# Moving the ending of the last state-space batch behind the phase boundary, and the first q and k loads in front of it

## The reference, cut to what matters

```
x1 = x  + layernorm(SSM(layernorm(x)))      # SSM: v + forward(v) + backward(v)
y  = x1 + layernorm(ATT(layernorm(x1)))     # ATT: attention, then 2 of 8 experts

forward(v): u, z = split(norm(v) @ Win.T); u = silu(conv4(u))
            dt, B, C from u;  h = exp(dt*A)*h + dt*u*B   (16 states, along the 512 positions)
            y = sum_n h_n*C_n + u*D;  out = (y * silu(z)) @ Wout.T
ATT(v):     q, k, v from rmsnorm(v); rope on q, k; 16 heads, 4 groups; causal softmax
            + residual; rmsnorm; router; the two chosen experts; + residual
```

## Times and profile before

| | us |
|---|---|
| median of 3 runs | 1732.66 |
| lowest, highest | 1731.58, 1736.15 |
| the profiled execution, its own time | 1733.05 |
| its span, from the first to the last instruction | 1731.3 |

### The profile page before, as it was taken

The page is one execution under the profiler, slowest core; times in us unless marked ns, Lnnn a source line. Parts: engine busy times, 40 slices in busy tenths (PEclk is TensorE's granted clock), DMA queues, the critical chain, the costliest instruction groups (busy, mean ns, idle before and its releaser), DMA issues. The chain is left out here.

```text
span 1731.3 us, 30902 instructions
## 1 busy us (share of the span) xinstructions
PE 1340.6 (77%) x8880; PEld 970.1 (56%) x8880; DVE 1387.3 (80%) x2234; ACT 1063.0 (61%) x1888; POOL 1109.6 (64%) x1244
## 2 busy tenths in 40 slices
PE   4878787778778787877787647798988889888671
PEld 2656566556656665656566423345665566556561
DVE  2999999999999999999999645676878777776422
ACT  6777676786776777767767215565655565546230
POOL 2777777787778777878777624454646666545435
PEclk8898899899899898998898768888999999999886
DMA  5112302320222023113203021134645545563672
GB/s 191 60 46 99 123 4 94 122 98 18 104 98 116 7 98 122 52 46 122 98 19 120 24 91 43 43 119 153 193 139 180 172 136 173 171 191 120 207 213 71
DMA packets 115418, 186.12 MB, mean 108 GB/s; under 512 B 10752, under 2 KB 87680, under 8 KB 111104
## 3 DMA queue, kind: packets, MB, share of 16 engines
q1 hardware_dynamic: 111200, 176.36, 29.6%
q0 software_dynamic: 4096, 8.40, 1.7%
HBM read 153.99 MB, written 26.15 MB: 104 GB/s over the span
## 5 line engine op out<-in xcount | busy, mean ns | idle before, releaser
L1021 POOL TENSOR_TENSOR hc<-hb,cb 128x512 f32<-128x512 f32 x512 | 653.9, 1296 | 199.1 <-DVE hb L873 168.9
L873 DVE TENSOR_TENSOR_SCAN hb<-da,dbu 128x512 f32<-128x512 f32 x448 | 527.7, 1205 | 16.8 <-PE dbu L440 8.7
L711 ACT ACTIVATE da<-dt,a_neg 128x512 f32<-128x512 f32 x512 | 351.5, 716 | 184.3 <-DVE hb L873 157.3
L477 PE MATMUL yp<-ident,hc 128*128 128x128 f32 x2048 | 322.6, 292 | 5.7 <-POOL hc L1021 5.3
L1967 ACT ACTIVATE pt<-scores,lift 128x512 f32<-128x512 f32 x320 | 216.3, 683 | 172.9 <-PE scores L1712 165.4
L477 PEld LDWEIGHTS yp<-ident,hc 128*128 128x128 f32 x2048 | 272.9, 153 | 87.0 <-issue 54.3
L2097 DVE TENSOR_REDUCE mx<-ms 128x1 f32<-128x384 f32 (+3 forms) x352 | 218.2, 636 | 103.7 <-PE ms L1674 96.6
L857 DVE TENSOR_TENSOR dbu<-dtu,bp 128x512 f32<-128x512 f32 x384 | 251.2, 684 | 14.1 <-PE bp L465 4.3
L2438 POOL TENSOR_SCALAR_AFFINE_SELECT pt<-pt 128x256 f32<-128x256 f32 (+1 forms) x320 | 118.2, 372 | 201.5 <-ACT pt L1967 199.6
L388 PE MATMUL wp<-xpad,wu 128*128 128x512 f32 x256 | 131.8, 606 | 11.6 <-DVE res L888 6.5
L1674 PE MATMUL ms<-k,q 72*128 72x384 bf16 (+3 forms) x512 | 137.2, 326 | 0.0
(11 more groups left out here) (251 smaller groups left out, 2398.5 us busy)
## 6 DMA issues: line engine op xcount, KB each, us to landing
cb<-c_scratch SPq DMA_DIRECT2D x16, 3072.0 KB, 11.7
wt<-ffn_w_e SPq DMA_DIRECT2D x120, 384.0 KB, 4.4
cb<-c_scratch SPq DMA_DIRECT2D x16, 1024.0 KB, 4.6
q<-q_scratch SPq DMA_DIRECT2D x96, 96.0 KB
xg<-xs_scratch SPq DMA_DIRECT2D x24, 256.0 KB, 3.4
ys_scratch<-ysb SPq DMA_DIRECT2D x24, 256.0 KB
q_scratch<-qp SPq DMA_DIRECT2D x21, 128.0 KB
k<-k_scratch SPq DMA_DIRECT2D x32, 72.0 KB
```

Source lines behind the costliest of these rows:

```text
L477: last = nc.tensor.matmul(yp[:, c, h * P:(h + 1) * P], src[:, c * P:(c + 1) * P], ident[:, :], is_transpose=True, start=(s < 0 and h == 0 ...
L711: nc.scalar.activation(da[:, s % NDA, :], dt[:, h, :], ACT.Exp, scale=a_neg[:, d, h, n:n + 1]).then_inc(da_done, 1)
L873: nc.vector.tensor_tensor_scan(hb[:, s % NHB, :], da[:, s % NDA, :], src, 0.0, ALU.mult, ALU.add).then_inc(scan_done, 1)
L1021: nc.gpsimd.tensor_tensor(hc[:, s % NHC, :], hb[:, s % NHB, :], cb[:, d, s // 2, :], ALU.mult).then_inc(hc_done, 1)
```

## The change

The ending of batch 7 leaves the state-space block and is called from the attention block by closures that `mamba_phase` returns. `ident`, `yp` and `wp` (as `ms`) are shared; `pa` and `po` are the two halves of `yp`; the tensors that the ending needs (sz, yg, ygt, wout, xres, res, x1t and others) lie in the space of the expert weights `wt`; `q9` and `k9` lie in one tensor with the C rows of direction 0, which the last unit does not read. q and k of batch 0 are loaded at the end of SP's program in the state-space block, and `k9` is set to ones in POOL's step 8 of the last unit. The FIRST_... constants are some 4 to 7 steps earlier.

```diff
-FIRST_IN = (8, 9)
-FIRST_RSTD = 10
-FIRST_NORM = (20, 22)
-FIRST_XT = 17
-FIRST_HT = 24
-FIRST_PROJ = (19, 19, 22)
-FIRST_ROPE = (20, 21, 24, 24)
-FIRST_ADD = (22, 27)
-FIRST_ACT = (29, 31, STEPS, STEPS)
-FIRST_POOL = (25, 29, 30, STEPS)
+FIRST_IN = (2, 4)
+FIRST_RSTD = 5
+FIRST_NORM = (13, 16)
+FIRST_XT = 11
+FIRST_HT = 19
+FIRST_PROJ = (13, 13, 16)
+FIRST_ROPE = (14, 15, 18, 18)
+FIRST_ADD = (16, 21)
+FIRST_ACT = (24, 27, 29, STEPS)
+FIRST_POOL = (19, 23, 24, 28)
+FIRST_ONES = 8
...
-        cb = sb("cb", [P, NDIR, NS, SEQ])
+        cb = (shared["qk"][:, :].bitcast(F32).rearrange("p (n s) -> p n s", n=NS), sb("cb", [P, NS, SEQ]))
+        win_u = hc[:, 0, :].rearrange("p (d n) -> p d n", d=NDIR)
...
-            sp.wait_ge(taps_folded, NDIR)
+            sp.wait_ge(xd_ready, count(xd_ready, NB - 1, 2))
             sp.dma_start(wq, ffn["wq"]).then_inc(ffn_loaded, 16)
...
             sp_first_store(sp)
-            sp_store(sp, NB - 1)
             sp.wait_ge(first_stored, 16 * 8)
-            sp.wait_ge(x1_stored, count(x1_stored, NB - 1, 16))
+            sp.wait_ge(hc_done, count(hc_done, NB - 1, STEPS))
+            for g in range(NKV):
+                qk_in(sp, q9, k9, ffn["q"], ffn["k"], g, g, first_loaded[g], first_ones)
...
             pe_unit(pe, NB - 1, 1, tail=(NB - 1, 0))
-            pe_ygt(pe, NB - 1, 1, last_unit=True)
-            for c in range(TC):
-                pe_out(pe, NB - 1, c)
...
             act_first(act, STEPS)
-            act_ygt(act, NB - 1, 1, 0)
-            act_ygt(act, NB - 1, 1, 1)
...
             dve_unit(dve, NB - 1, 1, tail=(NB - 1, 0))
-            dve_yg(dve, NB - 1, 1)
-            for k in range(4):
-                if k == 2:
-                    dve.wait_ge(end_step, count(end_step, NB - 1, 4))
-                dve_end(dve, NB - 1, k)
...
+            if s == FIRST_ONES:
+                pool.wait_ge(hc_done, count(hc_done, NB - 1, STEPS))
+                nc.gpsimd.memset(k9, 1.0).then_inc(first_ones, 1)
...
             pool_first(pool, STEPS)
-            pool_end_rstd(pool, NB - 1)
-            pool_x1(pool, NB - 1)
...
+LAST_X1 = -22
+def qk_in(sp, q9, k9, qscr, kscr, g, at, done, ones=None):
+    for a in range(3):
+        sp.dma_start(q9[a * 3 * HD:(a + 1) * 3 * HD, at].rearrange("r h s -> r (h s)"),
+                     qscr[a:a + 1, :, GH * g:GH * (g + 1)].rearrange("a d h s -> a d (h s)")
+                     .to_broadcast([3, HD, GH * SEQ])).then_inc(done, 16)
+    if ones is not None:
+        sp.wait_ge(ones, 1)
+    sp.dma_start(k9[0:PART_ROWS, at:at + 1].rearrange("r h s -> r (h s)"),
+                 kscr[:, :, g:g + 1].rearrange("b d h s -> b d (h s)").rearrange("b d n -> (b d) n")
+                 .unsqueeze(0).to_broadcast([3, 3 * HD, SEQ])).then_inc(done, 16)
...
+            if s == -34:
+                for dst, name in first_weights:
+                    sp.dma_start(dst[...], w[name]).then_inc(loaded, 16)
+            if s == -16:
+                for dst, name in rest_weights:
+                    sp.dma_start(dst[...], w[name]).then_inc(rest_loaded, 16)
+                ending["sp"](sp)                 # the store of x1 of batch 7
...
             for f, k in due("w", s):
+                if f == 0 and k == 0:
+                    ending["sp_stored"](sp)
...
-            sp.dma_start(ident[...], w["ident"]).then_inc(casts_loaded, 16)
...
+            if t % MAX_GROUP == 0 and is_first(b):
+                pe.wait_ge(ending["qk_loaded"][t // MAX_GROUP], 64)
...
                 if f == 0 and i == 0:
                     pe.wait_ge(casts, 2)
+                    ending["pe_wait_res"](pe)
                 pe_max(pe, f, i)
...
+            ending["pe"](pe)                     # ahead of the slots: pe_ygt, pe_out
+            ending["act"](act)                   # ahead of the slots: act_ygt twice
+            ending["dve"](dve, -1)               # ahead of the slots: dve_yg
...
+            if s == -30:                         # DVE, ahead of this slot's maxima
+                for k in range(3):
+                    ending["dve"](dve, k)
+            if s == LAST_X1:
+                ending["dve"](dve, 3)
...
+            if s == -30:                         # POOL
+                ending["pool"](pool, 0)
+            if s == LAST_X1:
+                ending["pool"](pool, 1)
...
-            nc.gpsimd.memset(k9[:, :, :], 1.0).then_inc(consts, 1)
```

More of the change, by code:

```diff
@@ L130, in sig, with part @@
             return s
-        ident = sb("ident", [P, P])
-        win_u = sb("win_u", [P, NDIR, DI])
+        NDA, NHB, NHC = 8, 4, 8
+        ident, yp, wp = shared["ident"], shared["yp"], shared["wp"]
+        taken = 0
+        def part(*shape):
+            nonlocal taken
+            names = " ".join("abcd"[:len(shape)])
+            n = int(np.prod(shape))
+            a = shared["wt"][:, taken:taken + n]
+            taken += n
+            return a.rearrange(f"p ({names}) -> p {names}", **dict(zip("abcd", shape)))
+        sz = part(NDIR, TC, DI)
+        yg = part(TC, DI)
+        ygt = part(NDIR, NH2, SEQ)
+        wout = part(NDIR, NH2, DM)
+        xres = part(2, TC, DM)
+        res = part(TC, DM)
+        x1t = part(TC, DM)
+        hb = part(NHB, SEQ)
+        dtt = part(TC, DI)
+        stats = part(2, TC, 6)
+        mv = part(2, TC, 2)
+        rstd = part(2, TC)
+        mhalf = part(2, TC)
+        eps = shared["wt"][:, taken:taken + TC]
+        q9, k9 = shared["q9"], shared["k9"]
         win_z = sb("win_z", [P, NDIR, DI])
@@ L1083, in _, with pe_last, pe_wait_res, act_last @@
             pool_first(pool, STEPS)
-            pool_end_rstd(pool, NB - 1)
-            pool_x1(pool, NB - 1)
+        def pe_last(pe):
+            pe_ygt(pe, NB - 1, 1, last_unit=True)
+            for c in range(TC):
+                pe_out(pe, NB - 1, c)
+        def pe_wait_res(pe):
+            pe.wait_ge(res_done, count(res_done, NB - 1, 1))
+        def act_last(act):
+            act_ygt(act, NB - 1, 1, 0)
+            act_ygt(act, NB - 1, 1, 1)
+        def dve_last(dve, k):
+            if k < 0:
+                dve_yg(dve, NB - 1, 1)
+            else:
+                if k == 2:
+                    dve.wait_ge(end_step, count(end_step, NB - 1, 4))
+                dve_end(dve, NB - 1, k)
+        def pool_last(pool, k):
+            if k == 0:
+                pool_end_rstd(pool, NB - 1)
+            else:
+                pool_x1(pool, NB - 1)
+        def sp_last(sp):
+            sp_store(sp, NB - 1)
+        def sp_last_stored(sp):
+            sp.wait_ge(x1_stored, count(x1_stored, NB - 1, 16))
+    return {"pe": pe_last, "pe_wait_res": pe_wait_res, "act": act_last, "dve": dve_last, "pool": pool_last,
+            "sp": sp_last, "sp_stored": sp_last_stored, "qk_loaded": first_loaded}
 NHEAD, NKV, HD = 16, 4, 8
@@ L1180, in last_plan @@
     return {}
-MADE_BEFORE = ("xa", "in", "in_rstd", "norm", "h0", "ht", "ht_copy", "rope", "qk_add", "part", "qk_part", "parts_out")
+MADE_BEFORE = ("xa", "in", "in_rstd", "norm", "h0", "ht", "ht_copy", "rope", "qk_add", "part", "qk_part", "parts_out", "parts_in")
+LAST_X1 = -22
[9 more added lines that the diff above has]
+                 .unsqueeze(0).to_broadcast([3, 3 * HD, SEQ])).then_inc(done, 16)
 def due_table():
@@ L1276, in sig @@
             return s
-        ident = sb("ident2", [P, P])
+        ident, q9, k9, ms = shared["ident"], shared["q9"], shared["k9"], shared["wp"]
+        wt = shared["wt"][:, :].rearrange("p (j n) -> p j n", n=WCOL)
+        pa, po = (shared["yp"][:, 2 * i:2 * i + 2, :].rearrange("p c n -> p (c n)") for i in range(2))
         identb = sb("identb", [P, P], BF16)
```

84 lines of the change are left out of this document (30 added, 54 removed).

## The result

| | before | changed |
|---|---|---|
| median of the first measurement (4 runs each) | 1732.12 | 1712.02 (1704.37 to 1724.04) |
| its ratio, 95% interval | | 0.9896 [0.9849, 0.9943] |
| profiled execution, its span | 1731.3 | 1704.9 |
| second measurement, 12 runs of the changed kernel | 1724.51 | 1723.84, ratio 1.0012 [0.9973, 1.0051] |
| third measurement, 12 runs | 1725.11 | 1719.45, ratio 0.9969 [0.9934, 1.0004] |

What follows compares the result with a forecast made beforehand. DVE bound the last unit, then the ending and the first q and k loads waited one after the other; -9.9 - 0.8 + 1.15 - 1.0 = -10.6 us on the profiled 1733.05, forecast 1722, range 1716 to 1728.5.

Steps and rivals of the forecast that it cites:

- Scan 27 ends near 975.15 as before: Last state-space unit: DVE does the same work and POOL makes its memset good, so zero cost on the path.
- The stall of 2.1 us in SP's issues: End of the state-space block: 16 q and k issues slowed by queued loads, between 0 and 5.1 us, taken as 2.1.
- They have 5 us of slack: Head of the attention block: ht, mask and xa, needed only at 10 us after its start, have 5 us to spare.
- slower: Rival, attention block's head: queued loads hold up xa, ahead of res; below 49 GB/s a loss, 1739 at 40; chance 0.05.
- DVE's first wait is xa beyond T + 9: Sign of a wrong prediction: DVE first waits for xa over 9 us after T, the attention block's start.
- less than 8 us earlier: Sign of a wrong prediction: batch 0's maxima in the attention block end less than 8 us earlier than before.
- x1t: Attention block, slot -22: DVE makes x1t between the maxima, 1.11 us, charged as +1.15.
- The clock: Attention block's head: product, v and scores without a gap may keep PE's clock up, 0 to 2.5 us, taken as -1.0.

Runs made afterwards that it cites:

- e1: The changed kernel measured again, nothing edited: median 1723.84 over 12 runs, ratio 1.0012 to the kernel before.
- e9: The changed kernel measured a third time, nothing edited: median 1719.45, ratio 0.9969 to the kernel before.
- e5: The changed kernel with batch 0's projections, rope products and adds one step later in the last unit: median 1711.18, ratio 0.9935 to the kernel before.
- e7: The changed kernel without early loads, projections, rope products and adds one step later, k9 set to ones in the attention block: median 1702.86, ratio 0.9885.
- e2: The changed kernel with ending, loads and FIRST_ constants back as before; shared buffers and step 8 memset stay: median 1723.43, ratio 0.9988 to the kernel before.
- e3: The changed kernel without its early loads; q and k loaded in the attention block as before: median 1709.41, ratio 0.9898 to the kernel before.
- e6: The changed kernel with only groups 0 and 1 of q and k loaded early, the others in the attention block: median 1712.66, ratio 0.9944.
- e4: The changed kernel with the ending back in the state-space block, q and k still loaded early: median 1719.82, ratio 0.9971 to the kernel before.
- e10: The changed kernel with projections, rope products and adds one step later and only two groups loaded early: median 1704.69, ratio 0.9896 to the kernel before.

## Why the prediction was wrong

In the direction it was right, also that the ending and the loads would overlap. As a time it was 10 us above the first reading; as a gain, 10.6 us, it was 6.5 above what the change is worth over all runs. The means of e1 and e9, 1723.2 and 1719.0, do lie in my range of 1716 to 1728.5, but by luck: I counted from a profile at 1733.05 and three runs near it, and before has a mean of 1724.1, so a base 9 us too high made up for a gain too large. Up to the first masked score it can be read step by step, in us after the mark:

| step | forecast | changed | difference |
|---|---|---|---|
| last k part issued | 70.45 | 75.11 | +4.7 |
| from there to the first q load | 2.35 | 2.07 | -0.3 |
| first q load to POOL's first instruction of the block | 15.07 | 13.20 | -1.9 |
| from there to the first masked score | 10.88 | 14.24 | +3.4 |
| first masked score | 98.75 | 104.62 | +5.9 |
| from there to the first scores | 25.5 | 26.0 | +0.5 |

(Before, POOL's first instruction stands at 1005.01, 0.92 after the block's first at 1004.09, so the forecast's 11.8 is 10.88 here, and its 14.15 for the loads 15.07.)

**"Scan 27 ends near 975.15 as before": the failed step.** I priced the last unit at zero because DVE's work was the same, and looked only at POOL's backlog. The order on PE was what mattered: 3.45 us of waiting for one dbu behind two projections, and 0.53 us for POOL's hc while it made good the memset. These are 4.0 of the 4.7 us; the other 0.7 were not traced. I had the rows that price a projection and did not ask what stood behind it on PE. The price has two values, 3.5 us where PE's clock is low there and 1.8 where it is full (e9). e5 removed the larger part (last scan 72.60), e7 all of it (71.41). The memset costs the 0.5 us only together with the earlier steps: in e2 it stands in the same step 8, the last scan is at 71.54, and POOL has no layer norm just ahead of it.

**The stall of 2.1 us in SP's issues** did not come. All sixteen went plain, at 2.10 to 2.25 for three q loads, near the 2.20 of the earlier trace rows:

```profile
977.01 2.25 SPq L1233 DMA_DIRECT2D qk<-q_scratch  x3
...
979.31 0.68 SPq L1238 DMA_DIRECT2D qk<-k_scratch  x1
980.03 2.10 SPq L1233 DMA_DIRECT2D qk<-q_scratch  x3
...
985.77 2.10 SPq L1233 DMA_DIRECT2D qk<-q_scratch  x3
987.92 0.68 SPq L1238 DMA_DIRECT2D qk<-k_scratch  x1
```

With it the stretch from the first q load to the block was forecast 1.9 too long. But it was the wrong question. Issuing costs SP 11.6 us at the end of the state-space block, where all five engines wait for it. In the attention block it costs no less (14 us before, one of the issues slow), but others hardly wait for it there: 1.2 to 1.3 us in e3 and e7.

**"They have 5 us of slack": the second failed step.** The mask, ht and xa of batch 1 landed 9.8 to 10.1 us after their issue. Before, ht took 2.8 and the mask 2.1. The issues with size and median us to landing, before (1004 to 1018), then changed (976 to 1010):

```profile
ht<-x_scratch SPq DMA_DIRECT2D x1, 256.0 KB, 2.8
...
mask<-ffn_mask SPq DMA_DIRECT2D x1, 128.0 KB, 2.1
```
```profile
GB/s 39 0 0 43 72 82 77 73 43 28 77 77 77 77 75 80 77 82 90 203 228 157 260 119 82 81 247 270 321 64 66 84 24 0 19 0 0 0 10 14
...
ht<-x_scratch SPq DMA_DIRECT2D x1, 256.0 KB, 9.8
xa<-x_scratch SPq DMA_DIRECT2D x1, 256.0 KB, 10.1
...
mask<-ffn_mask SPq DMA_DIRECT2D x1, 128.0 KB, 9.9
```

Each slice is 0.85 us: the loads move 72 to 82 GB/s until about 992, but for the slices at 43 and 28, and only then do other transfers show. My rival "slower" had this mechanism: DVE waits for xa ahead of res. I gave it a chance of 0.05 only with a rate under 49 GB/s, because I asked when it would turn the whole change into a loss, and charged nothing for it at the rate that I expected. At 77 it cost 2.9 us of the 3.4 in the table. The other 0.5 is yg, which started 1.70 us after T and not 1.2, with the queue or without it (1.68 in e6, 1.68 in e7). That the queue is the cause is shown by e6: with half of the loads ahead of them the mask landed 5.4 us after its issue and ht 5.3, and the 2.4 us came back. Of the signs that I had named, "DVE's first wait is xa beyond T + 9" came true: T is 989.3 and xa ended the wait at 1002.49. So did "less than 8 us earlier": the first scores, behind the maxima of the first groups, came 4.2 us ahead of before.
The Trainium skill (DMA: Bandwidth & Descriptors, "Why a DMA increments its semaphore by 16 and not by 1" and "Queues, rings and completion order") says that a load which uses k engines gets the lowest-numbered k, and that an engine takes its descriptors in ring order. By that all sixteen loads lie on the same three engines, and a later load over sixteen engines waits for its share on those. The landings of about 10 us agree, but no run here shows which engines a load used. I had used the Trainium skill there for the rate alone.

**x1t** cost DVE 1.11 us as forecast, in its place:

```profile
1008.61 1.11 DVE L911 TENSOR_SCALAR wt<-wt 128x128 f32<-128x128 f32 x4 [0.30 <-POOL wt L1000]
```

**The clock**, -1.0 forecast. The stretch to the first scores, 25.34 before, took 26.00, 26.18 and 29.6 in the three profiles. Less the 1.11 of x1t that it now holds, it was 0.3 to 0.5 shorter than before in two of them and 3.2 longer in the third. The mean clock in it was 0.66 before, and 0.67, 0.67 and 0.50 in the three. So the product, v and scores without a gap did not keep the clock up: in the first 17.6 us of the maxima it was 0.52, against 0.50 before. Whether the clock comes up there is open from run to run, so a single figure was the wrong form.

**What the first reading was.** By the means it was 19.6 us. Before's four runs were 9.0 above before's later mean, and the four of the change 8.0 below its own; 2.6 are left. The two profiles say the same. Of the 26.4 us between their spans, 7.4 lie ahead of the mark; 4.2 are the boundary; the other 14.8 lie behind the first scores. Behind the first scores before's profile takes 689.2 us, the longest of all thirteen. The changed kernel's three take 674.5, 678.0 and 675.1, and e2, which does before's work there in before's order, 675.6. So that part is spread of before's one profile and no gain. Ahead of the mark, e1, the same kernel as the changed one, comes 4.5 later than before, not 7.4 earlier (911.72 against 907.25). There one thing is open. The kernels that load q and k early have the mark at 899.8 to 900.8 in five profiles (the first one, e4, e5, e6, e10) and at 911.7 and 910.7 in two (e1, e9). Those that don't have it at 907.3 to 914.3 in all six. The early loads stand behind the mark in SP's program, and e1 and e9 show that they don't fix it; whether the edit has a hand in it all the same is not shown. What makes the loop fall into the one rhythm or the other, and why the time goes with the mean clock when raising it in one place did not lower it, is not settled.

## What to carry to other kernels

A transfer moved ahead of a barrier costs its issue on the path and its place in the queue for all that is issued behind it: ask what lands next, not only what lands earlier. When small pieces of work are put into a full loop, look at what stands behind them on each engine, above all at what the pacing engine waits for; "the same work, shifted" is no price of zero. And measure again before explaining, the kernel before too: four runs of each with a standard deviation of 7 us gave -20 for a change that all runs together put at -4, and 9 of the 20 were the kernel before.

## What the runs showed of the hardware

- Two profiles of one kernel differ by 11.9 us after 900 us (899.83 and 911.72) with a clock of 0.91 and 0.90, and the same 1203 to 1204 ns for a scan. 10.0 us of it is more idle time of DVE; PE's same 4161 matmuls took 11.9 us longer. Which of the two leads is not shown.
- PE at the low clock (0.50, 1.2 GHz) can stay there with PE busy 25.37 of 29.60 us (e9), while the same matmuls in two other runs of the same kernel got a mean of 0.67.
- The same two projections took 2.05 and 1.76 us in one run and 1.10 and 1.02 in another of the same kernel, and the wait behind them 3.45 and 1.8 us.
- Sixteen loads issued back to back did not slow SP (0.68 to 0.75 us each), though the mask issued behind them took 9.9 us to land. The slow issues came after them: xa, 1.13 us instead of the 0.43 in e6, and lnw, 3.14 us for 1 KB.
